# Pairwise attention pooling on one core: where TensorE does a block's Gram matrices, when the logits are copied, and how the result is stored

## What is computed

```python
row, col = np.triu_indices(F, k=1)                   # x: (2048, 39, 64)
ip = x[:, row, :] * x[:, col, :]                     # (2048, 741, 64)
hidden = relu(einsum('bpd,da->bpa', ip, W_w) + b_w)  # A = 64
logits = einsum('bpa,a->bp', hidden, W_h) + b_h[0]
a = softmax(logits, axis=1)[:, :, None]
y = sum(a * ip, axis=1) @ W_p + b_p                  # (2048, 1)
```

## Time and profile before

| | us |
|---|---|
| median of 3 runs | 1065.8 (1064.28 to 1067.39) |
| the profiled execution | 1061.95 |
| its span, first to last instruction | 1060.2 |
| TensorE busy | 1034.4 (98%) |
| VectorE busy | 983.1 (93%) |
| ScalarE busy | 871.3 (82%) |
| GpSimd busy | 827.9 (78%) |
| mean granted TensorE clock | 0.996 of full |

### The profile page before, as it was taken

How to read it: one execution, slowest core, us unless ns; L and a number is a source line. 1 busy time by engine, 2 the same in 40 slices (tenths; PEclk the granted TensorE clock), 3 DMA queues, 4 the chain that set the end, 5 groups by cost and what they waited for, 6 DMA issues and landing times.

```text
span 1060.2 us, 59040 instructions
## 1 busy us (share of the span) xinstructions
PE 1034.4 (98%) x24848; PEld 473.0 (45%) x24848; DVE 983.1 (93%) x485; ACT 871.3 (82%) x884; POOL 827.9 (78%) x327
## 2 busy tenths in 40 slices
PE   7999999999999999999999999999999999999995
PEld 3444455444444445444444454444444444544542
DVE  8899999999999999989999999999999999999990
ACT  5888888888888888888888888888888888888873
POOL 6897887858878688876879679786788868888790
PEclk9999999999999999999999999999999999999998
DMA  3134252432524324342342523325243243423422
GB/s 51 29 49 45 35 58 31 49 41 37 57 37 49 44 34 51 46 48 36 45 47 39 55 33 51 43 35 58 34 50 47 35 49 46 49 35 46 48 27 27
DMA packets 416138, 45.73 MB, mean 43 GB/s; under 512 B 416083, under 2 KB 416083, under 8 KB 416083
## 3 DMA queue, kind: packets, MB, share of 16 engines
q1 hardware_dynamic: 415695, 45.12, 34.8%
q10 hardware_dynamic: 388, 0.07, 0.0%
HBM read 26.59 MB, written 18.54 MB: 43 GB/s over the span
## 4 chain that ended last, share of the span: by engine, by line
PE 97%; issue 1%; ACT 1%; DMA 0%; DVE 0%; SPq 0%; DVEq 0%
PE z L543 61%; PE logits L579 31%; PE z L513 5%; ACT hidden L432 0%; DMA first_x_rows<-in_r_x_dram 0%; PE logits L569 0%; PE z L497 0%; ACT exps L455 0%; DVE neg_max L363 0%; DVE weighted L371 0%; SPq L228 0%; DVE exp_bias L365 0%; DVE y_all L377 0%; DVE inv_sum L374 0%; DVEq L376 0%
## 5 line engine op out<-in xcount | busy, mean ns | idle before, releaser
L432 ACT ACTIVATE hidden<-z,b_col 128x988 f32<-128x988 f32 x768 | 804.2, 1083 | 159.8 <-PE z L543 158.9
L354 DVE TENSOR_TENSOR prod<-x_wide 128x2964 f32<-128x2964 f32 (+1 forms) x257 | 848.0, 3349 | 8.3 <-PE z L543 1.7
L543 PE MATMUL z<-prod,w_tiles 64*32 64x494 f32 x12288 | 763.2, 576 | 0.0
L291 POOL COPY head_w<-head_cols 128x64 f32<-128x64 f32 x252 | 510.3, 2055 | 82.2 <-PE logits L579 80.2
L579 PE MATMUL logits<-hidden,head_w 64*32 64x371 f32 (+1 forms) x8192 | 444.0, 472 | 6.2 <-issue 4.9
L302 POOL TENSOR_SCALAR x_scaled<-x_wide,wp_col 128x624 f32<-128x624 f32 x64 | 314.1, 4907 | 125.9 <-DVE x_wide L330 120.0
L543 PEld LDWEIGHTS z<-prod,w_tiles 64*32 64x32 f32 x12288 | 251.0, 106 | 266.4 <-issue 223.6
L579 PEld LDWEIGHTS logits<-hidden,head_w 64*32 64x32 f32 x8192 | 173.7, 106 | 249.8 <-issue 242.6
L327 DVE STREAM_TRANSPOSE x_wide<-x_rows 128x1024 f32<-128x1024 f32 x63 | 78.5, 1246 | 36.0 <-PE z L513 32.6
L513 PEld LDWEIGHTS z<-x_wide,x_scaled 64*39 64x39 f32 x4096 | 45.3, 113 | 40.7 <-issue 40.6
L513 PE MATMUL z<-x_wide,x_scaled 64*39 64x39 f32 x4096 | 52.9, 204 | 1.5 <-ACT hidden L432 0.9
(11 more groups left out here) (23 smaller groups left out, 24.4 us busy)
## 6 DMA issues: line engine op xcount, KB each, us to landing
x_rows<-in_r_x_dram SPq DMA_DIRECT2D x252, 64.0 KB
gram<-gram_out SPq DMA_DIRECT2D x256, 47.5 KB
gram<-gram_out SPq DMA_DIRECT2D x256, 23.2 KB
values<-gram SPq DMA_DIRECT2D x128, 46.3 KB, 3.7
x_rows<-in_r_x_dram SPq DMA_DIRECT2D x252, 14.0 KB
first_x_rows<-in_r_x_dram SPq DMA_DIRECT2D x2, 78.0 KB
first_x_rows<-in_r_x_dram SPq DMA_DIRECT2D x1, 156.0 KB
out_dram<-y_all SPq DMA_DIRECT2D x8, 0.9 KB
```

Source lines behind the costliest of these rows:

```text
L291: nc.gpsimd.tensor_copy(head_w[:, step % BLOCK_STEPS, :, :], head_cols[:, :, at:at + TILE]).then_inc(head_w_ready, 1)
L354: nc.vector.tensor_tensor(out, one, other, ALU.mult).then_inc(ready, 1)
L432: nc.scalar.activation(hidden[:, i, :, CHUNK * k:CHUNK * (k + 1)], z[:, SLOT[j], :, 0:CHUNK], ACT.Relu, bias=b_col[:, 0:1]).then_inc(z_rea ...
L543: last = nc.tensor.matmul(z[col:col + TILE, SLOT[j], b, 0:CHUNK], w_tiles[row:row + D, col:col + TILE], prod[row:row + D, i, first:first + ...
```

## The change

- **The Gram matrices** move from between chunks 5 and 6 to between chunks 1 and 2, for all blocks but block 0, and take slot 2 of `z` in place of slot 0. The slots of chunks 2 to 5 change with them (`SLOTS`; block 0 has `FIRST_SLOTS`), and the waits are worked out by `reads_before` in place of the table. `cross_work` now waits for both its slots ahead of the Gram matrices.
- **One TensorE loop**: groups 0 to 15 are one pair of loops whose inner bound is `GROUP_BLOCKS - (g + 1) // GROUPS`, 63 blocks in all. Only block 63 is straight code.
- **The logits** are copied right after relu 4, ahead of relu 5 (before: after the Gram copy, ahead of relu 6).
- **The result**: `y_all` (128 x 16) is transposed by one matmul into 16 rows of 128, copied out of PSUM by VectorE with the columns put in order, and stored by one DMA of SP. All earlier stores of y are gone. `ident` grows from 103 x 39 to 128 x 128, made by one select in place of two.
- `b_col` and `wp_col` get semaphores of their own, and both loads of `b_col` are issued first.

The core of the diff:

```diff
-    CROSS_AT = CHUNKS // 2
-    LAST_CROSS_AT = 3
+    CROSS_AT, FIRST_CROSS_AT = 2, 6
 ...
-    SLOT = (1, 0, 2, 1, 0, 2, 1, 2, 0, 1, 0, 2)
-    EARLIER = (9, 10, 11, 0, 1, 2, 3, 5, "gram", 6, 8, 7)
-    GRAM_SLOT = 0
+    FIRST_SLOTS = (1, 0, 2, 1, 2, 0, 1, 2, 0, 1, 0, 2)
+    SLOTS = (1, 0, 1, 0, 2, 0, 1, 2, 0, 1, 0, 2)
+    GRAM_SLOT = 2
 ...
+    def reads_before(item, v):
+        everything = (*range(CHUNKS), "gram")
+        slot, at = slot_of(item, v), place(item, v)
+        same = [place(other, v) for other in everything if slot_of(other, v) == slot and place(other, v) < at]
+        if same:
+            return ITEMS * v + max(same) + 1
 ...
@@ sync @@
-                    if m == GROUP_BLOCKS - 1 and last:
-                        sp.wait_ge(y_ready, GROUPS - 1)
-                        for q in range(QUADS):
-                            for h in range(2):
-                                at = 32 * q + GROUP_STEPS * h
-                                sp.dma_start(y_dram[q, h, :, 0:GROUPS - 1], y_all[at:at + GROUP_STEPS, 0:GROUPS - 1],
-                                             allow_slow_non_contiguous=True).then_inc(early_y_stored, 16)
 ...
-            sp.wait_ge(y_ready, GROUPS)
-            for q in range(QUADS // 2):
-                store_last_y(sp, q)
-            sp.wait_ge(early_y_stored, 16 * 2 * QUADS)
-            sp.wait_ge(y_stored, 16 * QUADS)
+            sp.wait_ge(y_rows_ready, 1)
+            sp.dma_start(y_rows_dram, y_rows[:, :]).then_inc(y_stored, 16)
+            sp.wait_ge(y_stored, 16)
@@ vector @@
             pool_group(GROUPS - 1, 1, GROUPS // 2)
+            dve.wait_ge(y_turned, 1)
+            nc.vector.tensor_copy(y_rows[:, :].rearrange("g (t e) -> g t e", t=GROUP_STEPS),
+                                  z[0:GROUPS, 0, 0, 0:P].rearrange("g (e t) -> g t e", t=GROUP_STEPS)
+                                  ).then_inc(y_rows_ready, 1)
@@ scalar, block_work @@
                     if j == cross_at(v) - 1:
                         copy_gram(v, slot, writes)
-                        if ended is not None:
-                            copy_logits(ended)
+                    if j == 4 and ended is not None:
+                        copy_logits(ended)
@@ tensor @@
             def cross_work(v):
-                gram_matrices(v, prod_of=CROSS_AT // THIRDS)
-                chunk(v, CROSS_AT)
+                j = cross_at(v)
+                pe.wait_ge(x_scaled_ready, v + 1)
+                if j % THIRDS == 0:
+                    pe.wait_ge(prod_ready, BLOCK_STEPS * v + j // THIRDS + 1)
+                for item in ("gram", j):
+                    pe.wait_ge(z_read, reads_before(item, v))
+                nc.tensor.sem_inc(z_claimed, 1)
+                gram_matrices(v)
+                chunk(v, j)
 ...
                 second_half(v, 2)
-                chunks(2, 3)
+                if following:
+                    cross_work(v + 1)
+                chunks(3)
                 first_half(v, 3)
-                chunks(4, 5)
+                chunks(4)
                 second_half(v, 3)
-                if following and cross_at(v + 1) == CROSS_AT:
-                    cross_work(v + 1)
-                else:
-                    chunks(6)
-                chunks(7)
+                chunks(5, 6, 7)
 ...
-            with pe.Fori(0, GROUPS - 1) as g:
+            with pe.Fori(0, GROUPS) as g:
                 pe.wait_ge(logits_free, g + 1)
                 nc.tensor.sem_inc(z_claimed, 1)
                 open_logits()
-                with pe.Fori(0, GROUP_BLOCKS) as m:
+                with pe.Fori(0, GROUP_BLOCKS - (g + 1) // GROUPS) as m:
                     block_work(GROUP_BLOCKS * g + m)
-            pe.wait_ge(logits_free, GROUPS)
-            nc.tensor.sem_inc(z_claimed, 1)
-            open_logits()
-            with pe.Fori(BLOCKS - GROUP_BLOCKS, BLOCKS - 2) as v:
-                block_work(v)
-            block_work(BLOCKS - 2)
             block_work(BLOCKS - 1, following=False)
+            pe.wait_ge(y_ready, GROUPS)
+            nc.tensor.matmul(z[0:GROUPS, 0, 0, 0:P], y_all[:, :], ident[:, :],
+                             is_transpose=True, start=True, stop=True).then_inc(y_turned, 1)
```

More of the change, by code:

```diff
@@ L204, in write_gram @@
             def write_gram(v, slot):
[L205 removed]
+                sp.wait_ge(z_read, ITEMS * v + place("gram", v) + 1)
                 for u in range(2):
@@ L230, in _ @@
             for h in range(2):
-                rows = slice(h * D, (h + 1) * D)
-                sp.dma_start(b_col[rows, :], b_hidden.rearrange("(a o) -> a o", o=1)).then_inc(cols_loaded, 16)
-                sp.dma_start(wp_col[rows, :], w_out).then_inc(cols_loaded, 16)
+                sp.dma_start(b_col[h * D:(h + 1) * D, :],
+                             b_hidden.rearrange("(a o) -> a o", o=1)).then_inc(b_col_loaded, 16)
+            for h in range(2):
+                sp.dma_start(wp_col[h * D:(h + 1) * D, :], w_out).then_inc(wp_col_loaded, 16)
             sp.wait_ge(zeroed, 1)
@@ L280, in _ @@
             pool.wait_ge(ident_ready, 1)
-            for j in range(2):
-                one = ident[j * D:j * D + FIELDS, :]
-                nc.gpsimd.affine_select(out=one, in_=one, compare_op=ALU.not_equal, fill=1.0, base=0,
-                                        pattern=[[-1, FIELDS]], channel_multiplier=1).then_inc(ident_ready, 1)
-                pool.wait_ge(ident_ready, j + 2)
+            nc.gpsimd.affine_select(out=ident[:, :], in_=ident[:, :], compare_op=ALU.not_equal, fill=1.0, base=0,
+                                    pattern=[[-1, P]], channel_multiplier=1).then_inc(ident_ready, 1)
             def place_heads(step):
@@ L496, in transpose, with gram_matrices @@
                     duo = first_x_rows[rows, 2 * d:2 * d + 2, :].rearrange("f h d -> f (h d)")
-                    last = nc.tensor.matmul(z[:, slot, u, FIELDS * d:FIELDS * (d + 1)], duo, ident[rows, :],
+                    last = nc.tensor.matmul(z[:, slot, u, FIELDS * d:FIELDS * (d + 1)], duo, ident[rows, rows],
                                             is_transpose=True, start=True, stop=True, tile_position=(u * D, 0))
                 last.then_inc(x_cols_ready, 1)
-            def gram_matrices(v, prod_of=None):
-                pe.wait_ge(x_scaled_ready, v + 1)
-                if prod_of is not None:
-                    pe.wait_ge(prod_ready, BLOCK_STEPS * v + prod_of + 1)
-                before = item(BEFORE_GRAM) if cross_at(v) > BEFORE_GRAM else EARLIER[BEFORE_GRAM]
-                pe.wait_ge(z_read, ITEMS * v + before + 1)
-                nc.tensor.sem_inc(z_claimed, 1)
+            def gram_matrices(v):
                 for d in range(ROW_DUOS):
@@ L554, in hidden_layer @@
                     pe.wait_ge(prod_ready, BLOCK_STEPS * v + i + 1)
-                claim_slot(v, j)
+                before = reads_before(j, v)
+                if before is not None:
+                    pe.wait_ge(z_read, before)
+                elif j == 1:
+                    pe.wait_ge(act_spread, 2)
+                elif j == X_CHUNK:
+                    pe.wait_ge(x_spread, 2)
+                    pe.wait_ge(act_spread, 4)
                 nc.tensor.sem_inc(z_claimed, 1)
```

82 lines of the change are left out of this document (31 added, 51 removed).

## The result

| | before | after |
|---|---|---|
| median of 17 runs each, us | 1062.83 (1058.59 to 1068.34) | 1057.45 (1053.32 to 1061.01) |
| profiled execution / its span, us | 1061.95 / 1060.2 | 1055.1 / 1053.3 |

The change makes the kernel faster: ratio 0.9948, 95% interval 0.9929 to 0.9966. The forecast was 1053.8, range 1050.3 to 1061.0, so the sign and the range held. The forecast set out from the median of the first three runs, 1065.8, and took 12.0 us off; the 17 runs of the kernel before have 1062.83, and 5.4 us came off, a bit under half of the forecast gain.

A forecast was written before the change was run, and what follows sets the result against it. The prediction took TensorE, busy 98% of the span, as the bound. Gains of 5.2 (group starts), 2.0 (last blocks) and 5.2 (end), less 0.1, 0.2 and 0.1, made 12.0 us: 1053.8 us, range 1050.3 to 1061.

The forecast's parts named there:

- Start of a group: TensorE at 15 group starts: no more waiting for ScalarE's logits copy, 0.35 us each, 5.2 us gained (4.0 to 6.3).
- they are under matmuls if the queue is ahead: TensorE's queue each group: the new inner bound's few register instructions would be hidden under matmuls.
- first rival: Group starts gain nothing, since register work and branches replace the wait for the copy: 1059.0 us, chance 0.14.
- x_scaled: GpSimd's scaling of x, needed by the earlier Gram matrices: seldom late, by 0.4 us at most; +0.2 us (0 to 1).
- the window is passed, at most touched a few times: GpSimd's scale_x is late only for X between S - 0.3 and S + 0.1, which blocks would rarely meet.
- X - S: Start of VectorE's first multiply (X) against end of step 3's second half (S): from 1.0 down to about -3 us.
- second rival: GpSimd late with x_scaled in every block, 0.4 us each, 24 us slower in all: 1077.8 us, chance 0.10.
- SP's Gram stores go out some 4.5 us earlier: SP's queue: Gram stores leave earlier, loads of x still follow spread, so the queue only gains room; no cost.
- Gram matrices earlier, slots: TensorE's wait for freed PSUM slots ahead of the moved Gram matrices: a tie in 15 blocks, +0.1 us in all.
- Last blocks: Blocks 61 and 62 would run already-run loop code in place of straight code: 2.0 us gained (0.5 to 2.6).
- End: From last y_all to span end, 8.9 us before: transpose, copy and one DMA take 3.65, so 5.2 us gained.
- third rival: The final store into DRAM takes 6.9 us whatever its pieces: 1058.3 us, chance 0.09.

The follow-up runs named there:

- e4: Kernel before with only the logits copy moved ahead of the Gram copy: median 1056.03 us, ratio 0.9943.
- e8: Changed kernel with TensorE's loops of before (15 groups, constant inner bound, last group written out): median 1054.30 us, ratio 0.9915 to the kernel before.
- e13: Kernel before without the eight early stores of y: median 1059.34 us, ratio 0.9980.
- e7: Kernel before with only two edits, logits copied ahead of the Gram copy and y transposed and stored by one DMA: median 1046.25 us, ratio 0.9851.
- e1_y_only: Kernel before with only the new store of y (transpose, one DMA, no early stores): median 1053.88 us, ratio 0.9923.
- e11: Changed kernel with Gram matrices, order of halves and slots as before, logits copied behind relu 5: median 1052.27 us, ratio 0.9905 to the kernel before.

## Why the prediction was half right

**Start of a group: -5.2 forecast, -4.6 measured, with luck: two errors nearly cancel.** That the copy of the logits holds TensorE's queue was right (e4), and so was the lower end of "what remains is the 16 small matmuls, 0.25 to 0.40": 0.27 a start is left. The gain that this makes possible was put too low, at 0.35 a start with 0.42 as the upper end; it is 0.47, 7.0 us in all. The step "they are under matmuls if the queue is ahead", on the register work of the new bound, failed, and this failure is the second error (2.3 us): the queue isn't ahead there, as it stands at the wait for logits_free, and the instructions behind that wait are in the open. That is the first rival's mechanism, at 0.15 to 0.2 us a start (e8), not at the whole gain.

**x_scaled: +0.2 forecast, 1.6 in the profile (9 blocks).** The lengths held: issued in mid-multiply, scale_x takes two multiplies and 1.3 (7.91). That VectorE and GpSimd contend for SBUF, as the Trainium skill has it (SBUF — State Buffer, "Who interferes with whom"), agrees with 7.91 against 4.87 once the spread is held. The step that failed is "the window is passed, at most touched a few times": late by 0.4 at most was right, but X - S comes by the window in most groups. Counted from the start of the last matmul before S (0.47 ahead of its end), X is at +0.07 to +0.29 in the third block of 14 groups of 16, and mostly between -0.7 and -1.7 in the others; nine of the ten blocks are such third ones. X - S never ran on down to -3: it stays above -1.8, and each group brings it back by some 1.7 in the block where VectorE has the softmax work. The second rival (late in every block, 24 us) did not come.

**The missing term: about 4.4 us.** "SP's Gram stores go out some 4.5 us earlier ..., so its queue gains room" looked at the queue that issues and not at where the transfers end. Most of them now end around the handover between the halves of step 0, which has one chunk of cover, and the loads of x, which follow them on SP, start there. The trace of before had the clue, nine late signals, all with such a burst's end near and x being loaded; I hadn't looked for it, and no term of the sum held it.

**Gram matrices earlier, slots: +0.1.** Apart from x_scaled, they start late in 14 blocks by 3.1 us together, in 14 by 4.2 before: no loss.

**Last blocks: -2.0 forecast, -2.6 measured, wrong cause.** Not the straight code of block 62 (e8 has it and 43.3 us) but the early stores of y (e13, -2.3). The prediction named these stores, and put them at 0.

**End: -5.2 forecast, -6.3 measured.** The DMA and the close took 1.8 us from the start of the issue, where the sum put in 0.5 and 2.4. (Its 3.65 has no term of its own for the 0.5 that closes the program, which it had read from the trace; with it the forecast would have been 4.7.) So the DMA's term was too large even at its bound, the 2.3 of the small loads. The third rival is out. By the 2.0 us of fixed cost in the Trainium skill (DMA: Bandwidth & Descriptors, "Anatomy of one DMA — SWDGE (gpsimd) path") the end would have gained 5.6. That section gives the figure for a DMA that GpSimd issues, and this one is issued by SP; here issue, transfer and close together took less than that 2.0, so the measurement decides.

Summed: the parts that were the gain brought 15.8 us on their own (e7 by its ratio), and the rest of the change gave back about 10: 2.3 to 3.5 by the loop's bound, the rest by the Gram matrices' new place, in which 1.6 for x_scaled and 4.4 for late halves are seen in the profiles; the remaining 1 to 2 are not assigned.

## What to carry to other kernels

Price an earlier step by where its transfers end and which handover lies there, not only by the queue that they leave. A wait that keeps one engine from running ahead can be worth more than the wait that it avoids. Instructions behind a queue's wait are in the open, so a computed bound next to such a wait costs at every turn (0.15 to 0.2 us here). And when a change has five parts, the two cheap ones may hold all of the gain: try them alone.

## What the chip showed beyond that

- A semaphore signal of TensorE came at 0.54 to 0.56 us behind the last matmul's start in most cases, and at 0.75 to 2.5 us in 202 of 1,383 near the end of a burst of 156 and 76 byte packets (23% of the halves there while x was being loaded, 5% of the others there), never in 2,190 others.
- Eight stores of 4-byte pieces (about 2,000 packets in 5 us) cost TensorE 2.3 us that no semaphore explains (e13).
- The start depends on something that no edit here names. In e1_y_only TensorE enters its loop without a stall, in the changed kernel with 0.95 of "issue" in the midst of open_logits:

```profile
17.45 0.22 PE L554 MATMUL logits<-w_tiles 64*32 64x2 f32 x13
17.51 0.47 PE L564 MATMUL logits<-hidden,head_w 64*32 64x371 f32 x1
```
```profile
17.80 0.27 PE L559 MATMUL logits<-w_tiles 64*32 64x2 f32 x8
19.02 0.24 PE L559 MATMUL logits<-w_tiles 64*32 64x2 f32 x8 [0.95 <-issue]
```

  e11 has the short start too (30.8 us), the other kernels 32.3 to 33.7. TensorE's instructions are the same in e1 and e4 but for the last transpose and its ident, so where code or its transfers lie is a likely cause; it wasn't tried.
